# A mixture-of-experts router taken out of its own stage and spread over the attention and the first expert steps

## The reference

```
x = x + ln(attention(ln(x)))     # 16 heads, causal, low-rank queries (192) and keys/values (64)
x = x + ln(moe(ln(x)))           # the layer whose router is moved
x = x + ln(scan(ln(x)))          # gated linear recurrence
x = x + ln(qffn(ln(x)))          # feed-forward layer with whole-number weights and scales

def moe(h):
    scores = softmax(h @ gate_weight.T)            # 8 experts
    topk_w, topk_i = group_limited_topk(scores)    # best 2 of 4 groups of two, then best 2 of those
    wmat   = one_hot(topk_i) * topk_w              # a route per token and expert
    g, u   = h @ gate_w, h @ up_w                  # for each of 8 experts, 176 wide
    routed = sum_n wmat[:, n] * ((silu(g) * u) @ down_w)
    shared = (silu(h @ sh_gate) * (h @ sh_up)) @ sh_down
    return routed + shared
```

## Time and profile before

| | |
|---|---|
| three runs | 1802.36, 1805.91, 1807.36 us, median 1805.91 |
| the profiled execution's own time | 1806.03 us |
| its span in the trace | 1804.3 us |
| TensorE busy | 1608.8 us (89% of the span) |
| weight loads | 1318.3 us (73%) |
| VectorE busy | 1220.2 us (68%) |
| ScalarE busy | 1026.9 us (57%) |
| GpSimd busy | 302.1 us (17%) |

### The profile page before, as it was taken

How to read it: one execution, slowest core, us unless ns; L and a number is a source line. 1 busy time by engine, 2 the same in 40 slices (tenths; PEclk the granted TensorE clock), 3 DMA queues, 4 the chain that set the end, 5 groups by cost and what they waited for, 6 DMA issues and landing times. The chain is left out here.

```text
span 1804.3 us, 38201 instructions
## 1 busy us (share of the span) xinstructions
PE 1608.8 (89%) x14452; PEld 1318.3 (73%) x14452; DVE 1220.2 (68%) x2600; ACT 1026.9 (57%) x2017; POOL 302.1 (17%) x743
## 2 busy tenths in 40 slices
PE   3669999899999999999999999999965999988997
PEld 1357777777777777877887787787754778766886
DVE  3847766777677676777777777777746656576564
ACT  2336665666666566566666666656643435645573
POOL 3411112111211211121121121121110012020231
PEclk9879999999999999999999999999987999999999
DMA  8000000000000000000000000000011200000000
GB/s 231 1 0 2 2 2 1 2 2 1 1 2 1 2 2 2 1 1 2 2 2 1 2 2 1 2 1 2 2 26 49 81 0 1 1 19 21 1 21 27
DMA packets 27814, 23.54 MB, mean 13 GB/s; under 512 B 9692, under 2 KB 25180, under 8 KB 27508
## 3 DMA queue, kind: packets, MB, share of 16 engines
q1 hardware_dynamic: 22324, 14.77, 2.9%
q10 hardware_dynamic: 5312, 6.33, 1.2%
HBM read 19.00 MB, written 2.10 MB: 12 GB/s over the span
## 5 line engine op out<-in xcount | busy, mean ns | idle before, releaser
L697 ACT ACTIVATE pT_hi<-pT 128x512 f16<-128x512 f32 (+3 forms) x640 | 340.9, 533 | 366.7 <-PE pT L615 363.1
L818 DVE TENSOR_TENSOR pT_lo<-pT,pT_hi 128x512 f16<-128x512 f32 (+3 forms) x640 | 388.2, 607 | 159.1 <-ACT pT_hi L697 153.8
L806 DVE TENSOR_REDUCE cmx<-pS 128x1 f32<-128x512 f32 x576 | 347.9, 617 | 97.8 <-PE pS L602 94.2
L686 ACT ACTIVATE pr<-pS,nmx 128x512 f32<-128x512 f32 (+3 forms) x640 | 398.9, 623 | 11.1 <-DVE nmx L809 10.2
L615 PE MATMUL pT<-ident,pr 128*128 128x128 f32 x2176 | 346.2, 275 | 9.8 <-DVE pT_lo L818 6.9
L597 PE MATMUL pS<-lT_hi,qT_hi 128*128 128x512 f32 (+2 forms) x640 | 284.1, 444 | 57.9 <-ACT pr L686 49.0
L615 PEld LDWEIGHTS pT<-ident,pr 128*128 128x128 f32 x2176 | 258.2, 140 | 43.9 <-ACT pr L686 10.1
L657 PE MATMUL pO<-c_hi,pT_hi 128*128 128x65 f16 x2176 | 265.7, 194 | 1.2 <-DVE O L836 0.6
L658 PE MATMUL pO<-c_lo,pT_hi 128*128 128x65 f16 x2176 | 266.6, 193 | 0.0
L659 PE MATMUL pO<-c_hi,pT_lo 128*128 128x65 f16 x2176 | 263.7, 192 | 0.0
L602 PE MATMUL pS<-lT_hi,qT_lo 128*128 128x512 f32 (+2 forms) x640 | 257.4, 402 | 0.0
(11 more groups left out here) (243 smaller groups left out, 2510.0 us busy)
## 6 DMA issues: line engine op xcount, KB each, us to landing
X<-in_x SPq DMA_DIRECT2D x4, 512.0 KB, 6.8
wo<-in_w_o ACTq DMA_DIRECT2D x1, 2048.0 KB, 13.9
out<-X SPq DMA_DIRECT2D x8, 256.0 KB, 2.0
raw<-in_wd SPq DMA_DIRECT2D x14, 128.0 KB, 2.2
raw<-in_wg SPq DMA_DIRECT2D x13, 128.0 KB, 2.8
raw<-in_wu SPq DMA_DIRECT2D x13, 128.0 KB, 2.7
wqn<-in_w_qn ACTq DMA_DIRECT2D x1, 1536.0 KB, 17.6
raw<-in_qg SPq DMA_DIRECT2D x6, 128.0 KB, 2.5
```

Of the source, the lines that this page charges most:

```text
L686: act.activation(pr[:, at % RING, 0:n * P], pS[at % 4][:, 0:n * P], ACT.Exp, bias=nmx[:, p % 4:p % 4 + 1]).then_inc(sem("exped"), 1)
L697: act.activation(pT_hi[:, a % 4, 0:chunk[a][2] * P], src, ACT.Copy).then_inc(sem("t_hi"), 1)
L806: ch.inc(dve.tensor_reduce(cmx[:, p % 2, c:c + 1], pS[at % 4][:, 0:n * P], AX.X, ALU.max))
L818: dve.tensor_tensor(pT_lo[:, a % 4, 0:w], src, pT_hi[:, a % 4, 0:w], ALU.subtract).then_inc(sem("t_lo"), 1)
```

## The change

The router has no stage left, and one barrier of two goes with it. What it did is dealt out like this.

- **Transfers, first pieces.** At the attention's start SyncE loads the gate weights, the two gate vectors and the selector (in halves, through `raw`), then the first five pieces of expert weights into `raw`, and waits for them all. They aren't split there.
- **Constants.** Three steps at chunks 10, 14 and 18: the split of the gate weights and the row of small operations for `z`.
- **Logits by tile.** Two chunks behind a tile's `x_turn` TensorE makes its logits, with the turned tile as the stationary operand and 8 columns of gate weights moving: six matmuls, in a bank of `pT`. ScalarE copies them, VectorE takes the negated maximum, and two chunks later ScalarE takes the exponential with its sum.
- **Routes of the first half.** After the eighth tile: reciprocal of the sums, then six parts of the ranking, two chunks apart, then the turning of the routes.
- **Routes of the second half.** The same six parts in slots 5, 7, ... 15 of the expert steps, the turning in slot 20. Block 1's first step waits for the result.
- **`AHEAD` is 2, and no pieces are split beforehand.** `pieces(0)` and `pieces(1)` stand ahead of `up(0)` and `up(1)`, `pieces(m)` stands in slot 2(m-2), which is that of `up(m)`, behind `split(m-1)`. Every `up(m)` of block 0 waits for `w_lo`.

The router's buffers now live from the start; the statistics of the later layers use those of the attention again. The diff, cut to its core (`ch` is a chain by which one VectorE operation waits for the one before):

```diff
-AHEAD = 4
+AHEAD = 2
...
+            if part == 0:
+                step(dve.tensor_tensor(S_, S_, lsum[:, us].unsqueeze(2).to_broadcast([P, n8, NE]), ALU.mult))
+                step(dve.tensor_reduce(G[:, 0], pairs_, AX.X, ALU.max))
+                others_over_mine(G[:, 0], 4)
+            elif part == 1:
+                equal_ones_first(4)
+                rank(G[:, 1], 4)
+            elif part == 2:
+                ch.wait()
+                step(dve.tensor_tensor(M[:].rearrange("p t (g e) -> p t g e", e=2), pairs_, G[:, 1].unsqueeze(3).to_broadcast([P, n8, 4, 2]), ALU.mult))
+                others_over_mine(M[:], NE)
+            elif part == 3:
+                equal_ones_first(NE)
+            elif part == 4:
+                rank(R[:], NE)
+            else:
+                ch.wait()
+                step(dve.tensor_tensor(M[:], M[:], R[:], ALU.mult))
+                step(dve.tensor_copy(w3[:, :, 0:NE], M[:]))
+                step(dve.tensor_tensor(M[:], M[:], w3[:, :, 0:NE], ALU.subtract))
+                step(dve.tensor_copy(w3[:, :, NE:2 * NE], M[:]))
+                step(dve.tensor_tensor(M[:], M[:], w3[:, :, NE:2 * NE], ALU.subtract))
+                dve.tensor_copy(w3[:, :, 2 * NE:3 * NE], M[:]).then_inc(sem("l_split"), 1)
...
+                later_first = [[10, ("constants", 0)], [14, ("constants", 1)], [18, ("constants", 2)]]
+                later = list(later_first)
...
-                    for delay, step in ((2, "y_measure"), (4, "y_add"), (5, "x_measure"), (7, "x_norm"), (8, "x_turn")):
+                    for delay, step in ((2, "y_measure"), (4, "y_add"), (5, "x_measure"), (7, "x_norm"), (8, "x_turn"), (10, "logits"), (12, "l_exp")):
                         later.append([delay, (step, u)])
+                    if u == NT // 2 - 1:
+                        later.append([14, ("l_invert", 0)])
+                        for part in range(6):
+                            later.append([16 + 2 * part, ("route", (0, part))])
...
+                plan.append(("l_invert", 1))
+                t_kinds = ("probs", "o_turn", "x_turn", "logits", "route_turn")
...
+                        def logits(u):
+                            done = t_index["x_turn", u] + 1
+                            pe.wait_ge(sem("t_hi"), done)
+                            pe.wait_ge(sem("t_lo"), done)
+                            pe.wait_ge(sem("gw_lo"), 1)
+                            o = bank_t(("logits", u))
+                            sl = slice(tiles_in_order[u] * P, (tiles_in_order[u] + 1) * P)
+                            n = 0
+                            for k in range(KD):
+                                for a, w in ((lT_hi, gw_[0]), (lT_hi, gw_[1]), (lT_lo, gw_[0])):
+                                    m = pe.matmul(o[:, 0:NE], a[:, k, sl], w[:, k, :], start=(n == 0), stop=(n == 5))
+                                    n += 1
+                            m.then_inc(sem("t_turned"), 1)
+
+                        def route_turn(half):
+                            pe.wait_ge(sem("l_split"), half + 1)
+                            o = bank_t(("route_turn", half))
+                            turn_routes(pe, o[:].bitcast(BF16), half).then_inc(sem("t_turned"), 1)
...
+                            elif what == "logits":
+                                act.activation(L[:, a, :], src, ACT.Copy).then_inc(sem("t_hi"), 1)
...
+                            act.activation(S[:, u, :], L[:, u, :], ACT.Exp, bias=lmax[:, u:u + 1], accum_out=lsum[:, u:u + 1]).then_inc(sem("l_exped"), 1)
...
+                            if step == "constants" and at:
+                                pool.wait_ge(sem("sel_in"), 16 * at)
+                                pool.tensor_copy(selb[:, (at - 1) * FR // 2:at * FR // 2], sel_half).then_inc(sem("sel_ready"), 1)
...
+                            elif what == "logits":
+                                dve.tensor_reduce(lmax[:, a:a + 1], src, AX.X, ALU.max, negate=True).then_inc(sem("t_lo"), 1)
...
+                        def l_invert(half):
+                            dve.wait_ge(sem("l_exped"), (half + 1) * NT // 2)
+                            us = slice(half * NT // 2, (half + 1) * NT // 2)
+                            ch.inc(dve.reciprocal(lsum[:, us], lsum[:, us]))
...
+                        for k in range(2):
+                            if k:
+                                sp.wait_ge(sem("sel_ready"), k)
+                            sp.dma_start(sel_half, sel[:, k * FR // 2:(k + 1) * FR // 2]).then_inc(sem("sel_in"), 16)
+                        sp.wait_ge(sem("sel_ready"), 2)
+                        first_pieces = [wg[:, :, 0:P], wu[:, :, 0:P], wd[:, 0], wg[:, :, P:2 * P], wu[:, :, P:2 * P]]
+                        for n, src in enumerate(first_pieces[:SLOTS]):
+                            sp.dma_start(slot_of(raw, (src,), n), src).then_inc(sem("w_in0"), 16)
+                        sp.wait_ge(sem("w_in0"), 16 * SLOTS)
...
+            for part in range(6):
+                at_slot(5 + 2 * part, "route", (1, part))
+            at_slot(20, "route_turn", 1)
...
-            plan = [("up", 0), ("up", 1), ("gate", 0), ("split", 0), ("gate", 1)] + [step for slot in slots for step in slot]
+            plan = [("pieces", 0), ("up", 0), ("pieces", 1), ("up", 1), ("gate", 0), ("split", 0), ("gate", 1)] + [step for slot in slots for step in slot]
...
-                        if kind == "moe" and tb == 0 and m >= AHEAD:
+                        if kind == "moe" and tb == 0:
...
+                        if kind == "moe" and tb == 1 and m == 0:
+                            pe.wait_ge(sem("t_hi"), hi_read["route_turn", 1])
+                            pe.wait_ge(sem("t_lo"), lo_read["route_turn", 1])
...
-                        if n >= SLOTS:
-                            sp.wait_ge(sem("w_lo"), n - SLOTS + 1)
+                        if n < SLOTS:
+                            continue
+                        sp.wait_ge(sem("w_lo"), n - SLOTS + 1)
```

More of the change, by code:

```diff
@@ L165, in build @@
         weights = whole.enter_context(ExitStack())
+        raw = sb(whole, "raw", [P, SLOTS, D])
+        selb = sb(whole, "selb", [3 * NE, FR], BF16)
+        wT = sb(whole, "wT", [3 * NE, T], BF16)
+        z = sb(whole, "z", [P, 6, KD])
+        lbh = sb(whole, "lbh", [P, 2, KD])
+        gw_ = [sb(whole, f"gw_{k}", [P, KD, NE], F32R) for k in range(2)]
+        tri = sb(whole, "tri", [P, NE, NE])
+        L = sb(whole, "L", [P, NT, NE])
+        S = sb(whole, "S", [P, NT, NE])
+        lmax = sb(whole, "lmax", [P, NT])
@@ new lines, in build, with route, step, others_over_mine @@
+        lsum = sb(whole, "lsum", [P, NT])
+        w3 = sb(whole, "w3", [P, NT // 2, 3 * NE], BF16)
+        tiles_in_order = [t for k in range(NT // 2) for t in (NT - 1 - k, k)]
+        def route(dve, ch, half, part):
+            M, R, G, a, b = (small[name] for name in ("M", "R", "G", "a", "b"))
+            n8 = NT // 2
+            us = slice(half * n8, (half + 1) * n8)
+            S_ = S[:, us, :]
+            pairs_ = S_.rearrange("p t (g e) -> p t g e", e=2)
+            def step(ins):
+                ch.inc(ins)
+                ch.wait()
+            def others_over_mine(src, n):
+                mine, other = src.unsqueeze(3).to_broadcast([P, n8, n, n]), src.unsqueeze(2).to_broadcast([P, n8, n, n])
+                dve.tensor_tensor(a[:, :, 0:n, 0:n], other, mine, ALU.is_gt)
+                ch.inc(dve.tensor_tensor(b[:, :, 0:n, 0:n], other, mine, ALU.is_equal))
+            def equal_ones_first(n):
+                ch.wait()
+                ch.inc(dve.tensor_tensor(b[:, :, 0:n, 0:n], b[:, :, 0:n, 0:n], tri[:, 0:n, 0:n].unsqueeze(1).to_broadcast([P, n8, n, n]), ALU.mult))
+            def rank(dst, n):
+                ch.wait()
+                step(dve.tensor_tensor(a[:, :, 0:n, 0:n], a[:, :, 0:n, 0:n], b[:, :, 0:n, 0:n], ALU.add))
+                step(dve.tensor_reduce(dst, a[:, :, 0:n, 0:n], AX.X, ALU.add))
+                ch.inc(dve.tensor_scalar(dst, dst, 1.5, None, ALU.is_lt))
+            if part == 0:
[6 more added lines that the diff above has]
+            elif part == 2:
+                ch.wait()
+                step(dve.tensor_tensor(M[:].rearrange("p t (g e) -> p t g e", e=2), pairs_, G[:, 1].unsqueeze(3).to_broadcast([P, n8, 4, 2]), ALU.mult))
[5 more added lines that the diff above has]
+            else:
+                ch.wait()
+                step(dve.tensor_tensor(M[:], M[:], R[:], ALU.mult))
[4 more added lines that the diff above has]
+                dve.tensor_copy(w3[:, :, 2 * NE:3 * NE], M[:]).then_inc(sem("l_split"), 1)
@@ new lines, in turn_routes, with routes_at @@
+        def turn_routes(pe, bank, half):
+            us = range(half * NT // 2, (half + 1) * NT // 2)
+            for k, u in enumerate(sorted(us, key=lambda v: tiles_in_order[v])):
+                mm = pe.transpose(bank[0:3 * NE, k * P:(k + 1) * P], w3[:, u - us[0], :], identb[:])
+            return mm
```

(14 more changed lines are left out.)

266 lines of the change are left out of this document (92 added, 174 removed).

## The result

The changed kernel takes 1834.14 us in the median of four runs (1831.89 to 1836.31), the kernel before 1805.66 us beside it. The ratio is 1.016, with a 95% interval of 1.0138 to 1.0182. The profiled execution spans 1834.5 us, 30.2 more than before.

A forecast was written before the change was run, and what follows sets the result against it. TensorE bounds both sides of the router, itself a hole held by a VectorE chain. Step 13 starts 3.1 us later despite the removed 35 us; plus attention 19.2 and clock 6.4: 1806.0 + 28.7 = 1834.7 us, range 1815 to 1850.

The forecast's parts named there:

- The chain of the pieces: Expert steps 2 to 13: matmuls wait for VectorE's split weights, 7.0 us per routed step, 6.2 unrouted; 80.4 us in all.
- The clock: Expert steps: TensorE idles 2.2 us at a time, four falls to the low clock, 6.4 us, between 0 and 18.
- Start of the experts: After the barrier: step 0 starts 1.5 us later, step 2's pieces are done at 13.1 us, where step 2 began at 8.0.
- The tail: Attention's end: last tiles' logits, copy, maximum, exponential and reciprocal add 3.9 us, between 2 and 6.
- The attention: Attention before its last tiles: the router work dealt into it adds 19.2 us, between 5 and 36.
- The logits: Attention, 14 tiles: six 8-column matmuls each plus waits for a pT bank, 13 us, between 3 and 24.
- The first half's ranking and turning: Attention, on VectorE: six ranking parts on 8 tiles add 3.5 us, the turned routes 0.7.
- The constants: Attention, chunks 10 to 18: a VectorE chain of 14 instructions, 2.7 us at a stretch, adds 2 us.
- Pieces in time: Expert steps: with inputs ready early, steps stay at 4.75 us without gaps, total 1799 us; chance 0.05.
- VectorE can't carry the additions: Attention: VectorE bursts stop TensorE for long, so attention adds 42 us, total 1858 us; chance 0.05.
- Cheap attention, steady clock: Attention's waits swallow most added work, leaving 9 us, and the clock doesn't fall: 1818 us; chance 0.22.
- The clock falls in every gap: Expert steps: 12 falls of the clock in place of 4, adding 13 us, total 1848 us; chance 0.13.

The follow-up runs named there:

- the experiment on the constants: Changed kernel with the row of small VectorE operations for z dealt over five steps at chunks 18 to 26 instead of one: 1832.6 us, ratio 1.0139.
- the first experiment: Changed kernel with AHEAD = 3 and pieces(2) behind gate(0), so pieces stand one step further ahead: 1794.09 us, ratio 0.9939.

## Why the prediction was right, step by step

It was right: 1834.7 predicted, 1834.1 measured, and the forecast mechanism is the one that the runs show. The agreement to half a microsecond is partly luck. Step 13 was to start 28.7 us later than before, at 1467.4, and starts at 1467.44, but four terms missed and cancel: the attention 2.9 us less than forecast, the tail 0.1 less, the start of step 2 1.4 more, the steps with their clock 1.6 more. A fall of the clock at 1467 makes step 13 itself 1.5 us longer than before, where the prediction had no difference left, and the profiled run is 2.1 us above the median of the four.

**The chain of the pieces.** Right, and proven alone in both directions. A clean step takes 7.10 us where 7.0 was worked out, an unrouted one 6.2 to 6.3. Steps 2 to 13 were put at 80.4 us and the clock at 6.4, together 86.8; they measured 88.4, and 81.7 without most of the falls. Clean steps alone would make 9 x 7.10 + 6.3 + 6.2 = 76.4, and step 2's low clock 1.3, so the second half's ranking and turning took 4.0 us (forecast 5.0).

**The clock.** The size was near (8.0 us measured, 6.4 forecast), the count of falls not. Four falls behind the gaps were expected. The trace has two right at step 2 and 3, then ones at 1406, 1436, 1454 and 1467. That is six at 1.3 us, where the sum had four at 1.6. The gaps behave alike only on average: in the kernel before with `AHEAD = 2`, eleven gaps of 1.7 to 2.1 us brought one fall. The Trainium skill (TensorE: Matmul & The Clock Gate, HAM oscillation) tells of a loop in which every burst behind a wait starts at the low clock. Here the clock is low at the start, or falls within 1.5 us of it, in six of twelve bursts and in one of eleven, so taken as a rule for every gap it would have overstated the loss.

**Start of the experts.** VectorE ends the attention and then splits the first pieces:

```profile
1363.06 0.20 DVE L1008 RECIPROCAL lsum<-lsum 128x8 f32<-128x8 f32 x1 [0.46 <-ACT S L840]
1365.01 1.77 DVE L158 TENSOR_TENSOR W_all<-raw,W_all 128x256 fp32r<-128x256 f32 x5 [1.75 <-ACT W_all L154]
```

Step 0 begins at 1366.15, 1.6 us behind the barrier at 1364.5 (forecast 1.5). Step 2 begins 14.5 us behind it, 13.1 forecast. Most of the missed part is step 0, which ran wholly at the low clock and took 5.7 us (its first matmul at 1366.15, that of step 1 at 1371.89), not 4.65.

**The tail.** Forecast 3.9 us: the attention's last VectorE work stands at 1363.26, 20.1 us later than the earlier trace rows, of which 16.3 lie before the tail. That leaves 3.8.

**The attention.** Forecast 19.2 us before the tail, measured 16.3. The start of the scores of chunks 8, 26, 346, 366 and 586 (of 640), before:

```profile
134.94 0.47 PE L597 MATMUL pS<-lT_hi,qT_hi 128*128 128x512 f32 x1 [0.15 <-ACT pr L686]
...
167.37 0.50 PE L597 MATMUL pS<-lT_hi,qT_hi 128*128 128x512 f32 x1
...
779.51 0.47 PE L597 MATMUL pS<-lT_hi,qT_hi 128*128 128x512 f32 x1 [0.43 <-ACT pr L686]
...
816.12 0.47 PE L597 MATMUL pS<-lT_hi,qT_hi 128*128 128x512 f32 x1 [0.43 <-ACT pr L686]
...
1224.96 0.48 PE L597 MATMUL pS<-lT_hi,qT_hi 128*128 128x512 f32 x1
```

After:

```profile
131.67 0.47 PE L690 MATMUL pS<-lT_hi,qT_hi 128*128 128x512 f32 x1 [0.15 <-ACT pr L798]
...
169.94 0.54 PE L690 MATMUL pS<-lT_hi,qT_hi 128*128 128x512 f32 x1
...
786.19 0.48 PE L690 MATMUL pS<-lT_hi,qT_hi 128*128 128x512 f32 x1
...
824.15 0.50 PE L690 MATMUL pS<-lT_hi,qT_hi 128*128 128x512 f32 x1
...
1241.24 0.48 PE L690 MATMUL pS<-lT_hi,qT_hi 128*128 128x512 f32 x1
```

The differences are -3.3, +2.6, +6.7, +8.0 and +16.3. They are read like this:

- The logits cost 12.4 us for the 14 tiles ahead of chunk 586 (16.3 less 2.6 less 1.3 for the ranking). Forecast 13. The parts come out near the forecast's 10.1, 5 and 2 off as well: 84 matmuls at 0.11 us are 9.2 us, the waits ahead of them, from 200 to 1320 us, are 6.3, and the wait for the exponentials is 38.5 us where it was 42.4.

```profile
PE pS L690 <- ACT pr L798: 38.5, 101, 2.0
...
PE pT L736 <- DVE pT_lo L958: 4.3, 7, 1.0
...
PE pT L736 <- ACT pT_hi L809: 2.0, 4, 0.7
```

- The first half's ranking and turning cost 1.3 us (from 6.7 to 8.0), forecast 4.2. This term was mis-sized, and its working was at fault too: 7.7 us in six parts, each with 0.9 free, leave 2.3 and not 3.5. The parts stand two chunks apart, and TensorE lost less than even that.
- The constants cost 5.8 us (from -3.3 to +2.6), forecast 2. This was mis-sized the other way. The row, 16 operations and not 14, was put at 2.7 us with a quarter of VectorE's time free; it takes 3.4 us, TensorE idles 4.57 us, and then the clock falls for steps of the attention too. The working had looked for falls of the clock only among the experts.
- The -3.3 us are no work of the change. The profile of before has two falls of the clock at 123 and 130 us, that of after none there. Where they are present in both (the experiment on the constants), the difference is +0.3; where they are missing from the kernel before itself (its version with `AHEAD = 2`, whose attention is the same), it is -3.0. So the change's own work in the attention is 16.3 + 3.3 = 19.6 us, against the 19.2 forecast: the constants' 3.8 too little and the ranking's 2.9 too much cancel, and the forecast's 2.9 us miss above is the luck of one profile.

**Removed.** The 35.0 us of the stage are gone as forecast. The kernel with the pieces further ahead shows the account without the chain: 35.0 less 20.1 for attention and tail and less 2.8 for the later start of step 2 behind the barrier (10.8 us in place of 8.0) is 12.1, and it measured 12 us less than before.

**The rivals.** *Pieces in time* was the one that would have ended faster, at 1799 with all costs of the attention in; the experiment that makes it true measured 1794, since its attention cost 2.9 us less and its step 2 started 2.3 us earlier than that sum had them. Its point of decision, 5.3 us a step, can't be placed better: the runs have 4.73 and 7.10 and nothing between. *VectorE can't carry the additions* put the attention at 42 us; it cost 16.3, and the first experiment shows that VectorE has room in the expert steps as well. *Cheap attention, steady clock* fails on both counts: the attention cost 16.3 us and not 9, and the clock fell. *The clock falls in every gap* had twelve falls at 19 us; the trace has six at 8.

## What to carry to other kernels

When a stage is dissolved, look first at what it did on the side. Here the router's 35 us also hid the split of twelve pieces of weights, and without that cover the split stood behind each step's last VectorE operation, ahead of the next step's first matmul: a circle through three engines. Lay out such a loop and add up its longest chain (product, low part, pieces, matmuls) against the step's time on the bound engine; a distance of one more step in the order was worth 40 us, where moving the router was worth 12. And a row of tiny dependent operations left TensorE idle and then at the low clock, though TensorE was the bound; dealt out, 4.4 us came back in the trace.
